# Four states instead of two in each of GpSimd's C products, in a Mamba layer with an FP4 feed-forward

## The reference, cut to what matters

```python
# first: a selective state space layer, 4 heads x 128 channels x 16 states
xz = norm(x) @ in_proj_w.T;  x, z = split(xz)
x = silu(causal_conv4(x) + conv_b)                      # "uu" below
dt_r, B, C = split(x_proj(x))                           # per head, 16 + 16 + 16
delta = softplus(dt_proj(dt_r) + dt_proj_b)
for t in range(1024):                                   # for each channel d and state n
    s[d, n] = s[d, n] * exp(delta[d] * A[d, n]) + delta[d] * x[d] * B[n]
    y[d] = sum_n s[d, n] * C[n]
x1 = residual + ((y + x * Dskip) * silu(z)) @ out_proj_w.T
# second: a gated feed-forward, 256 -> 704 -> 256, every operand rounded to FP4 in blocks of 16
h = silu(q(v) @ q(w_gate).T) * (q(v) @ q(w_up).T),  v = norm(x1)
out = x1 + q(h) @ q(w_down).T                           # q: scale by the block's maximum / 6, round
```

## Time and profile before

| | before |
|---|---|
| timed runs, median (lowest to highest) | 4095.38 us (4092.26 to 4097.22) |
| profiled execution | 4092.62 us, its span 4090.5 us |
| TensorE matmul | 3967.5 us busy, 97%, x20652 |
| VectorE | 3967.9 us, 97%, x5426 |
| ScalarE | 3672.5 us, 90%, x6935 |
| GpSimd | 3939.0 us, 96%, x2461 |
| GpSimd's C products L762, 128x1024 | 1024 of 2370 ns mean, 2420.4 us |
| mean clock of TensorE | 0.995 of full speed |
| DMA | 772.86 MB, 58.5% of 16 engines on the one queue |

### The profile page before, as it was taken

One profiled execution on the slowest core, in us unless ns is written; L12 is line 12 of the kernel. 1 busy time (PEld: TensorE's weight loads), 2 busy tenths in 40 slices (PEclk: granted clock), 3 DMA queues, 4 the chain that ended last, 5 costly groups with the idle time before them and its releaser, 6 DMA issues. The chain is left out here.

```text
span 4090.5 us, 68836 instructions
## 1 busy us (share of the span) xinstructions
PE 3967.5 (97%) x20652; PEld 1972.0 (48%) x20652; DVE 3967.9 (97%) x5426; ACT 3672.5 (90%) x6935; POOL 3939.0 (96%) x2461
## 2 busy tenths in 40 slices
PE   4899999999999999999999999999999999999998
PEld 1234544544544545545544545545545544544545
DVE  6999999999999999999999999999999999999994
ACT  4899999999999999999999999999999999999875
POOL 5999999999999999999999999999999999999993
PEclk8999999999999999999999999999999999999999
DMA  3666666666656665665665656655665666566560
GB/s 104 211 208 192 196 196 189 201 194 193 200 193 192 201 193 191 201 195 189 200 197 187 202 194 190 200 194 192 198 196 193 196 197 194 195 197 193 192 190 22
DMA packets 307414, 772.86 MB, mean 189 GB/s; under 512 B 37734, under 2 KB 89062, under 8 KB 307046
## 3 DMA queue, kind: packets, MB, share of 16 engines
q1 hardware_dynamic: 305616, 767.03, 58.5%
q10 hardware_dynamic: 1430, 1.44, 0.2%
HBM read 743.16 MB, written 25.17 MB: 188 GB/s over the span
## 5 line engine op out<-in xcount | busy, mean ns | idle before, releaser
L762 POOL TENSOR_TENSOR prod<-state,cs 128x1024 f32<-128x1024 f32 x1024 | 2420.4, 2370 | 45.4 <-DVE state L1008 44.1
L987 DVE TENSOR_TENSOR db<-db,du 128x512 f32<-128x512 f32 x1408 | 958.5, 681 | 25.7 <-PE db L1062 25.5
L492 ACT ACTIVATE decay<-delta,aneg 128x512 f32<-128x512 f32 x1408 | 959.6, 715 | 20.7 <-DVE state L1008 20.3
L1077 PE MATMUL ybank<-prod,ident 64*64 64x512 f32 x3584 | 883.7, 605 | 12.1 <-POOL prod L762 9.9
L1077 PE MATMUL cross<-prod,ident 64*64 64x512 f32 x3584 | 883.7, 604 | 0.0
L1008 DVE TENSOR_TENSOR_SCAN state<-decay,carry,db 128x512 f32<-128x512 f32 x704 | 874.6, 1258 | 0.0
L1008 DVE TENSOR_TENSOR_SCAN state<-decay,db 128x512 f32<-128x512 f32 x704 | 833.6, 1200 | 0.1
L753 POOL TENSOR_TENSOR brow<-brow,du 128x512 f32<-128x512 f32 x640 | 824.0, 1288 | 3.3 <-PE bank_b L1345 3.1
L1062 PE MATMUL db<-pieces,sel 128*128 128x512 bf16 x1408 | 539.9, 384 | 34.0 <-DVE state L1008 32.1
L492 ACT ACTIVATE db<-delta,aneg 128x512 f32<-128x512 f32 x640 | 439.4, 687 | 8.0 <-DVE state L1008 6.4
L1077 PEld LDWEIGHTS ybank<-prod,ident 64*64 64x64 f32 x3584 | 205.9, 132 | 422.3 <-issue 333.4
(11 more groups left out here) (150 smaller groups left out, 7663.8 us busy)
## 6 DMA issues: line engine op xcount, KB each, us to landing
cs<-c_rows SPq DMA_DIRECT2D x1024, 512.0 KB, 3.8
brow<-b_rows SPq DMA_DIRECT2D x640, 256.0 KB, 4.1
xin<-in_hidden SPq DMA_DIRECT2D x128, 128.0 KB, 3.7
xres<-in_hidden SPq DMA_DIRECT2D x128, 128.0 KB, 4.4
out_x<-ot SPq DMA_DIRECT2D x128, 128.0 KB, 3.7
c_rows<-xdbl SPq DMA_DIRECT2D x128, 32.0 KB, 1.6
b_rows<-xdbl SPq DMA_DIRECT2D x128, 32.0 KB, 1.7
win<-in_win_t SPq DMA_DIRECT2D x1, 1024.0 KB, 8.0
```

Of the source, the lines that this page charges most:

```text
L492: act.activation(out, delta[:, w.mod(2), :], ACT.Exp, scale=aneg[:, w.mod(HEADS), n:n + 1]).then_inc(done, 1)
L762: pool.tensor_tensor(prod[:, r, :, :], state[:, 2 * p:2 * p + 2, :], cs[:, c, :, :], ALU.mult).then_inc(weighted, 1)
L987: dve.tensor_tensor(t[:, :], t[:, :], du[:, gu % 2, :], ALU.mult).then_inc(db_done, 1)
L1077: last = pe.matmul((ybank, cross)[k][c * Q:(c + 1) * Q, :], ident[rows, rows], prod[rows, p % P_RING, k, :], start=(p == 0), stop=(k == 1 ...
```

## The change

GpSimd's `weigh` takes four states and four rows of C in one instruction of 128 x 2048, four times a unit in place of eight. `cs` is two buffers of four rows (before: three of two), each filled by two DMAs of two rows, both of which wait until the buffer is free. `weighted` therefore counts products of four. The products still go into the ring of four pairs, two pairs at a time. `uu` has two buffers in place of four; the SiLU that writes one waits for du, x_proj and, by the new semaphore `d_mm`, the D product of one unit back in place of du and x_proj of three units back. The slots of all engines and the order of lines within a step are new, and so is the order of the DMAs. The count of instructions changes on GpSimd alone.

```diff
-PAIRS = NST // 2
-C_RING = 3
+PAIRS, QUADS = NST // 2, NST // 4
+C_RING = 2
 P_RING = 4
...
-        cs = sb("cs", [C_RING, 2, CH])
+        cs = sb("cs", [C_RING, 4, CH])
-        uu = sb("uu", [4, CH])
+        uu = sb("uu", [2, CH])
...
             def spread_c(u, p):
-                i = u.val(PAIRS, p)
+                i = u.val(QUADS, p // 2)
                 if p == 0:
                     sp.wait_ge(c_written, u.val(16, 16))
                 wait(sp, weighted, i + 1 - C_RING)
                 rows = c_rows[u.mod(2), 2 * p:2 * p + 2, :].rearrange("n c -> (n c)")
-                sp.dma_start(cs[:, i % C_RING, :, :].rearrange("p n c -> p (n c)"),
+                part = slice(p % 2 * 2, p % 2 * 2 + 2)
+                sp.dma_start(cs[:, i % C_RING, part, :].rearrange("p n c -> p (n c)"),
...
-                    wait(act, du_done, v.val(plus=-3))
-                    wait(act, xd_mm, v.val(plus=-3))
-                    act.activation(uu[:, v.mod(4), :], pbank[:, :], ACT.Silu, bias=cb[:, h:h + 1]).then_inc(u_done, 1)
+                    wait(act, d_mm, v.val(plus=-1))
+                    wait(act, du_done, v.val(plus=-1))
+                    wait(act, xd_mm, v.val(plus=-1))
+                    act.activation(uu[:, v.mod(2), :], pbank[:, :], ACT.Silu, bias=cb[:, h:h + 1]).then_inc(u_done, 1)
...
-            def weigh(w, p):
+            def weigh(w, q):
-                i = w.val(PAIRS, p)
-                c, r = i % C_RING, p % P_RING
-                pool.wait_ge(scanned, w.val(NST, 2 * p + 2))
-                wait(pool, c_landed[c], 16 * (i // C_RING + 1))
-                wait(pool, summed, w.val(PAIRS, p + 1 - P_RING))
-                pool.tensor_tensor(prod[:, r, :, :], state[:, 2 * p:2 * p + 2, :], cs[:, c, :, :],
-                                   ALU.mult).then_inc(weighted, 1)
+                i = w.val(QUADS, q)
+                c, r = i % C_RING, 2 * q % P_RING
+                pool.wait_ge(scanned, w.val(NST, 4 * q + 4))
+                wait(pool, c_landed[c], 32 * (i // C_RING + 1))
+                wait(pool, summed, w.val(PAIRS, 2 * q + 2 - P_RING))
+                pool.tensor_tensor(prod[:, r:r + 2, :, :].rearrange("p a b c -> p (a b) c"),
+                                   state[:, 4 * q:4 * q + 4, :], cs[:, c, :, :], ALU.mult).then_inc(weighted, 1)
...
-                if w := due("scan", 17):
-                    weigh(w, 7)
+                if w := due("scan", 15):
+                    weigh(w, 3)
...
-                    pe.wait_ge(weighted, w.val(PAIRS, p + 1))
+                    pe.wait_ge(weighted, w.val(QUADS, p // 2 + 1))
```

More of the change, by code:

```diff
@@ L1226, in side @@
                     spread_b(w.val(NST, 13))
-                if v := due("pre", 11):
-                    in_proj(v, 1, 1).then_inc(z_mm, 1)
-                if t := due("post", 73):
+                if w := due("scan", 6):
+                    spread_b(w.val(NST, 7))
+                if t := due("post", 30):
+                    pe.wait_ge(v_quant, t.val(plus=1))
+                    if peeled and t.val() == 0:
+                        pe.wait_ge(xnt_done, 11)
+                    else:
+                        wait(pe, h_op, t.val(2))
+                    for k in range(KM):
+                        last = pe.transpose(bank_b[:, k * P:(k + 1) * P], v2_eps[:, k * P:(k + 1) * P], ident[:, :])
+                    last.then_inc(v_tp, 1)
+                if t := due("post", 38):
+                    gate(t, 1, (0, 1))
+                if v := due("pre", 22):
+                    pe.wait_ge(pieces_done, v.val(plus=1))
+                    pe.matmul(pbank[:, :], dtws[:, v.mod(HEADS), :], xdbl[:, :],
+                              start=True, stop=True).then_inc(dt_mm, 1)
+                if t := due("post", 72):
+                    down(t, (2, 3))
+                if v := due("pre", 8):
+                    in_proj(v, 0, 1).then_inc(x_mm, 1)
+                if w := due("scan", 8):
+                    spread_b(w.val(NST, 9))
+                if t := due("post", 72):
                     down(t, (4, 5))
@@ L1277, in side @@
-                if v := due("pre", 20):
-                    pe.wait_ge(mid_done, v.val(plus=1))
-                    pe.matmul(pbank[:, :], less[:, 1, :], mid[:, :], start=False, stop=True,
-                              skip_group_check=True).then_inc(res_mm, 1)
-                if t := due("post", 29):
-                    pe.wait_ge(v_quant, t.val(plus=1))
-                    if peeled and t.val() == 0:
-                        pe.wait_ge(xnt_done, 11)
-                    else:
-                        wait(pe, h_op, t.val(2))
-                    for k in range(KM):
-                        last = pe.transpose(bank_b[:, k * P:(k + 1) * P], v2_eps[:, k * P:(k + 1) * P], ident[:, :])
-                    last.then_inc(v_tp, 1)
@@ L1290, in side @@
-                if w := due("scan", 13):
-                    spread_b(w.val(NST, 15))
-                if w := due("scan", 1):
-                    spread_b(w.val(NST, 2))
+                        last = pe.matmul(cross[others, :], ddiag[rows, w.mod(HEADS), :], uu[rows, w.mod(2), :],
+                                         start=False, stop=False, tile_position=(r * Q, (1 - r) * Q),
+                                         skip_group_check=True)
+                if w:
+                    last.then_inc(d_mm, 1)
```

561 lines of the change are left out of this document (274 added, 287 removed).

## The result

| | before | after |
|---|---|---|
| timed runs, median (lowest to highest) | 4094.2 us (4092.0 to 4097.2, 6 runs) | 4129.6 us (4125.9 to 4130.3, 6 runs) |
| profiled execution, its span | 4092.62, 4090.5 | 4130.31, 4128.2 |
| GpSimd's C products | 1024 of 2370 ns | 512 of 4538 ns |

The changed kernel takes 1.0082 times the time of before, 95% interval 1.0072 to 1.0093. The direction was the forecast one. The size was not: 4105 was predicted, with 4080 to 4124 for 8 in 10.

What follows compares the result with a forecast made beforehand. A circle of waits closing once per unit, from scan 15 to scan 15, was taken as the bound: 15 trips x 0.78 = +11.7, start -2.2, sum +9.5 us. Forecast 4105 us, 4080 to 4124 for 8 in 10.

Steps and rivals of the forecast that it cites:

- The product of four: On GpSimd, four states in one instruction take 4.50 us in place of 4.64 for two products.
- The order of waits, from scan 15 to scan 15: Closed circle over GpSimd, ScalarE, TensorE and VectorE, once a unit; an early unit can't be shorter than about 30.65 us.
- The test I had named: New profile: TensorE's first in_proj matmul waits for `delta` about 0.3 us in each unit, and VectorE waits for B row 12.
- in_proj k=0, 0.86: TensorE's first in_proj step after `delta` frees `pbank`, counted in the circle of waits at 0.86 us.
- Cost 0, with 0.7 us of cover: B row 4's DMA, behind C rows and xin, lands before GpSimd wants it at 35.2 us; upper end +0.3 a unit.
- Some tenths more: Allowance for B row 4's DMA: it lands in 4.1 us or some tenths more, at 34 to 34.5 in the unit.
- Rival 3: Much slower: B row 4 lands late, or ScalarE comes late to `v_eps`; 0.3 us per unit is 36 us, 4140; chance 0.1.
- Rival 1: Faster: the circle of waits is not closed and VectorE's early-unit waits go; 4069 at best, half gives 4083; chance 0.2.
- Late units: Units that start from a carry, with scans 0.06 us longer: 30.96 us, against VectorE's own 30.90.
- `uu` in two buffers, cost 0: SiLU(x) waits for D product, du and x_proj of one unit back; these end early enough, so cost 0.
- The start, -2.2 us: About four first units without feed-forward work go at GpSimd's pace and gain 4 x 0.56 = 2.2 us.
- ScalarE's 0.3 us: ScalarE is ready for `v_eps` about 0.3 us before `ve`; any lack adds in full to the circle of waits.

Runs made afterwards that it cites:

- run 5: Changed kernel with rstd (`ve`) ahead of the scaling of `hh` on GpSimd and the DMA of B row 4 ahead of the first C rows; 4089.3 us.
- run 6: Changed kernel with each product of four split into two of two states, and the DMA of B row 4 ahead of the first C rows; 4088.2 us.
- run 7: Changed kernel with TensorE's first in_proj product back behind the four down matmuls, and the DMA of B row 4 ahead of the first C rows; 4090.5 us.
- run 1: Changed kernel with the DMA of B row 4 issued ahead of the unit's first C rows on the sync queue; 4112.4 us.
- run 9: run 5 with VectorE's reciprocal of h's scales moved from behind scan 1 to ahead of scan 0; 4093.3 us.
- run 11: run 9 with the scales of h, which the reciprocal reads, one scan earlier on VectorE; 4084.6 us.
- run 10: Kernel before with only two buffers of SiLU(x) in place of four, with the changed kernel's waits; 4094.9 us.
- run 8: Kernel before, slots kept, with products of four states, two C buffers of four rows and two SiLU(x) buffers; 4301.3 us.
- run 2: Changed kernel with rstd (`ve`) ahead of the scaling of `hh` on GpSimd; 4093.9 us.
- run 4: Changed kernel with rstd (`ve`) directly behind the product of scans 12 to 15, and the DMA of B row 4 ahead of the first C rows; 4169.1 us.

## Why the prediction was right in its mechanism and wrong in its size

- **The product of four**: 4.50 was taken, the step is 4.50 (1890.13 to 1894.63). The Trainium skill's figure, GPSIMD Engine Reference, section 3.1, is 4497 ns; read as a duration, it stands against 4538 in the trace, the mean of 512. The row of the trace decides; either would have given the same forecast within 5 us.
- **The order of waits, from scan 15 to scan 15**: right at every handover. `ve` comes 7.15 behind the scan in the forecast, and 1897.21 - (1888.84 + 1.21) = 7.16 in the trace. The test I had named, TensorE waiting for `delta` and VectorE for row 12, is there; the view lists 15.2 us in 48 waits for the first, and the constant 0.14 us behind `delta` shows it in the other units too. Runs 5, 6 and 7 show that this is what costs.
- **The term "in_proj k=0, 0.86"**: mis-sized. It takes 0.94 (1902.62 to 1903.56). I had its price from a pair that stood behind other matmuls. A pair right behind a wait lasts 1.10 and not 1.02, and this could be read from the row shown at the earlier trace rows. (Of its two passes the first steps on after 0.50 us in all these units of the changed kernel, and after 0.43 in run 5, where it starts 0.23 us behind `delta`.) 0.08 in the circle, 120 times, is 9.6 us of the miss.
- **"Cost 0, with 0.7 us of cover" for B row 4**: the step that failed most. I had the place, the queue ahead of it and, within 0.13 us, the time of issue right: counted 0.85 + 0.07 ahead of the product of four, 0.79 in the unit shown. The landing was wrong. 4.1 was the median over all rows before; row 4 alone had 3.6 there. Behind 512 KB of C rows, and with 0.9 MB more issued within 1.5 us, it is 5.5 in the unit shown and 5.2 in the median of row 4, up to 6.4. The wait came to 18.9 us, of which run 1 gives back 17.2. "Some tenths more" should have been a whole microsecond. The Trainium skill, DMA: Bandwidth & Descriptors, section Latency and other measured facts, puts the access to HBM at 0.2 us on average and 2 us at high load. That fits the direction, but no run here separates it from queueing.
- **Rival 3**, in its first half, was therefore not a rival at 0.1 but part of what happened. Its second half, ScalarE late to `v_eps`, did not happen: `v_eps` starts 0.03 to 0.04 us behind `ve` in all 109 units looked at between 500 and 3900 us. The rival was priced at 0.3 in every unit, 36 us; it came as 40 waits of up to 1.1 us.
- **Rival 1** was right in that opening the circle makes the kernel faster, and wrong in how much. I gave 4069 to 4083; with the circle open the same order gives 4089. I had let VectorE's waits vanish with the circle. In run 5 an early unit takes 30.61, not the 30.20 that VectorE alone would need. VectorE still waits for B rows there, and TensorE shows almost no wait of its own; that TensorE's sum is the bound is read from the trace and was not tried by a run.
- **Late units**: 30.96 forecast, 31.02 to 31.04 in the trace, the same 0.08. Behind it a second small loss was hidden which I had not looked for, VectorE's new order (runs 9 and 11).
- **`uu` in two buffers, cost 0**: right, run 10. **The start, -2.2 us**: near in size by luck. The first trip is 3.8 us shorter, but I had given GpSimd's relief by the fused products as the reason, and in run 6, which has none, the first trip is 4.3 shorter (227.9). The gain belongs to the new order.

Put together: +11.7 forecast for the circle, +10 more for its length, +18.9 for late rows, -2.4 for the ends, 38.2 against 37.7 measured. Of the two thin covers, ScalarE's 0.3 us held and the row's 0.7 us did not. The range had no room for it: its upper end, 4124, was a circle longer by 0.15, and a late row stood only as the rival at 4140.

## What to carry to other kernels

When instructions are fused, the last part's wait moves ahead of the whole, and all that is queued behind on that engine moves with it; find the circle that this closes and every way out of it, not the one you know (run 8), and cut it by moving the small instruction that others wait for (run 2), but no further than its own inputs allow (run 4). A median landing time is no cover for a DMA that is issued behind a large one: take the latency at that place in the queue, and issue first what is wanted first. Price an instruction by a row in which it stands where it will stand, behind a wait or behind its kind.

## What the runs showed of the hardware

- B row 4, 256 KB, took 5.2 us to land in the median when issued behind 512 KB of C rows (changed kernel), 3.6 in the kernel before, and 3.5 in run 1, where it is issued first.
- An fp32 pair of in_proj whose start a wait decided lasted 1.10 us (1902.62), and 1.02 behind other matmuls (1905.28).
- On VectorE an instruction of 44 columns whose result the next one reads stepped on after 0.21 us in place of 0.09. A scan right behind a reciprocal took 1.10 from start to start (1748.30 to 1749.40); one behind a multiply, 1.19 (1746.79 to 1747.98).
